# Written-out sequence loops, statistics further ahead in the first and last stage, and a re-placed bias scaling and normalisation in the second attention

## The chip, the cores and the metric

One core of a Trainium2 chip runs the whole program. TensorE (PE) multiplies and transposes, VectorE (DVE), ScalarE (ACT) and GpSimd (POOL) do elementwise work and reductions, SyncE (SP) issues most of the DMAs. Each engine runs its own instruction stream in order; semaphores join them. The metric is the time of one execution on the device in microseconds, the median of several.

## The reference

Sixteen sequences of 256 tokens with 256 features go through six residual steps of a decoder:

```python
x = x + _L0_attn_ref(_layernorm(x), ...)      # decaying linear attention
x = x + _L0_xattn_ref(_layernorm(x), ctx, ...)  # causal attention, 16 heads
x = x + _L0_ffn_ref(_layernorm(x), ...)       # 8 experts, 2 per token
x = x + _L1_attn_ref(_layernorm(x), ...)      # time mix and channel mix
x = x + _L1_xattn_ref(_layernorm(x), ctx, ctx, fside, ...)
x = x + _L1_ffn_ref(_layernorm(x), weight, bias)
```

The second attention adds a bias to its scores, and the last step multiplies in 8-bit precision:

```python
scores = jnp.einsum('bhqd,bhkd->bhqk', Q, K) * SCALE
scores = scores + lambda_bias * bias_struct[:, None, :, :]
attn = jax.nn.softmax(scores, axis=-1)
...
x_mat = quantize_e4m3(x2d, SCALE).astype(jnp.float16)
w_mat = quantize_e4m3(weight, SCALE).astype(jnp.float16)
out2d = (x_mat @ w_mat.T).astype(jnp.float32) * (SCALE * SCALE) + bias
```

`_layernorm` subtracts the mean and divides by the root of variance + 1e-5; the first step also divides its output by the root of its mean square.

## The kernel before

X, all 16 sequences, stays on the chip from the first stage to the last: 128 partitions by 32 tiles of 256 features, two tiles per sequence. Each of six functions is one stage (`decay_attention`, names `dec_`; `causal_attention`, `xa_`; `experts_ffn`, `moe_`; `time_channel_mix`, `mix_`; `biased_attention`, `xb_`; `float8_ffn`, `ffn_`), begun by a barrier of all engines. There is no planner: the order on each engine is the order in which the code stands, and every wait is written out as a semaphore and a count. b is the sequence, s = b % 2 its buffer.

**Loops.** The generator `turns` (L123) gives the sequences to each engine: sequence 0 is written out, then a device loop `Fori` runs over pairs, and the last ones are written out again (three, for the stages below). `long_turns` (L449) does the same for the two attentions: 0 and 1 and the last two are written out, six passes of the loop take 2 to 13. Inside a device loop, counts and addresses come from registers.

**First stage.** VectorE's turn b: `norm(b + 2)` (L112), `scan(b + 1)` (L406), the copy of the sums of squares of b (L425), `measure(b + 3)` (statistics L95, aggregation L98), then, when GpSimd's root `rms` is there, the addition into X (L430). GpSimd computes the roots in two steps (`inverse_root`, L104 an addition, L106 a power): first that of `rms`, then that of the statistics, `rstd`. Statistics and roots have one buffer, so `norm(b + 3)` of the next turn needs the root of what was measured in this one. TensorE turns the input (L321), sums squares (L332) and projects (L336).

**Second attention.** A turn has four steps g of four units (a unit is two heads of a block of 128 queries). TensorE: `scores` of step g (L1271), one or two jobs for the next sequence on the shared bank `p_a` (turn context, turn x, project keys, queries, values), `turn_unit` of the four units of the step before (L1283), `sum_units` (L1301). VectorE: per unit `shift_unit` (L1510: subtracts the scaled bias `neg` and finds the extreme, two operations each with its read of the result), `copy_unit` (L1519), and the closings: `normalise` (L1527, L1531: gives `xb_o` and frees `p_a`, for which TensorE waits at step 3 before `project_values`, L1237), `measure` and `norm` of the sequence after next at step 2, `finish_keys`, `finish_values` (L1496). ScalarE: exponentials (L1436) and copies. `prepare` on GpSimd (L1186) makes `neg` from the loaded bias, one sequence ahead; `add` (L1191) puts the result into X.

**Last stage.** VectorE first quantises the weight in twelve steps (L2765 to L2776); TensorE turns it, ScalarE copies it. Then VectorE's turn b: `norm(b + 2)` (L2786, waits for the root), `quantise(b + 2)` (two casts, L2790 and L2793), `measure(b + 3)`, and the bias addition for b (L2810). GpSimd's turn: the root of b + 3, then the addition of b into X (L2691). TensorE turns the quantised input (L2707) and multiplies (L2716); ScalarE reads both (L2738, L2745). Four DMAs write X out as sequences 4, 9, 13 and 15 are added.

## Time and profile before

| | us |
|---|---|
| median of 3 runs (2154.88 to 2162.77) | 2159.51 |
| the profiled execution | 2163.67 |
| its span | 2161.6 |
| `dec`, 0 to 109.2 | 109.2 |
| `xa`, to 450.0 | 340.8 |
| `moe`, to 1085.0 | 635.0 |
| `mix`, to 1581.5 | 496.5 |
| `xb`, to 2061.9 | 480.4 |
| `ffn`, to the end | 99.7 |

Busy times over the span: PE 1737.4 us (80%), DVE 1265.4 (59%), ACT 1116.1 (52%), POOL 591.5 (27%). In `xb` PE is busy for 427.8 of 480.4 us; in `ffn` for 26.5 of 99.7, at a granted clock of 0.50, with DVE busy for 67.3 and POOL for 38.4. A busy share of the whole span says little here, since each stage has its own limit; stage by stage one reads the timeline of an engine, where the number in brackets is the time that the engine was idle before the row and what ended that.

### The profile page before, as it was taken

The numbers are of one execution on the slowest core, as the hardware profiler recorded it, in microseconds if no ns is written. First come the engines' busy times: TensorE is split into PE (matmuls) and PEld (weight loads), VectorE is DVE, ScalarE is ACT, GpSimd is POOL, SyncE is SP. The second block draws the span as 40 slices with busy tenths as digits, with TensorE's granted clock in tenths as the row PEclk, the third lists the DMA queues.
The fourth block names the chain that finished last, engine by engine and source line by source line (L and its number), as shares of the span: only waits on it lengthen the run. The fifth ranks groups of instructions, "written<-read, shape, count | busy, mean of one in ns | idle before, by whom it ended". The sixth has DMA issues, their size and how long they took to land. (4 is left out here: it accounts for less than half of the span.)

```text
span 2161.6 us, 44295 instructions
## 1 busy us (share of the span) xinstructions
PE 1737.4 (80%) x13555; PEld 1431.1 (66%) x13555; DVE 1265.4 (59%) x4307; ACT 1116.1 (52%) x2535; POOL 591.5 (27%) x752
## 2 busy tenths in 40 slices
PE   4747777755599999999926999999958999999822
PEld 3625555545488888889915777777737777777711
DVE  4759998846410110101118999999618777778656
ACT  1259999931122222223325666666518888888712
POOL 2333233221211111101024666666410111111024
PEclk9879999965699999999967999999969999999955
...
DMA packets 112598, 153.61 MB, mean 71 GB/s; under 512 B 11449, under 2 KB 96769, under 8 KB 112353
## 3 DMA queue, kind: packets, MB, share of 16 engines
...
## 5 line engine op out<-in xcount | busy, mean ns | idle before, releaser
L1895 ACT ACTIVATE moe_hT<-moe_p_h,moe_b 128x256 f32<-128x256 f32 (+1 forms) x344 | 131.8, 434 | 370.8 <-PE moe_p_h L1845 370.6
L1845 PE MATMUL moe_p_h<-moe_gT,moe_w 128*128 128x256 f32 (+1 forms) x1376 | 256.9, 345 | 0.8 <-issue 0.8
L1855 PE MATMUL moe_p_y<-moe_w,moe_hT 128*128 128x256 f32 x1136 | 252.3, 379 | 0.0
L1845 PEld LDWEIGHTS moe_p_h<-moe_gT,moe_w 128*128 128x128 f32 x1376 | 228.2, 192 | 25.9 <-issue 1.2
L1436 ACT ACTIVATE xb_pr<-xb_sc,xb_nmax 128x256 f32<-128x256 f32 x512 | 225.5, 502 | 25.3 <-DVE xb_nmax L1510 23.2
L1855 PEld LDWEIGHTS moe_p_y<-moe_w,moe_hT 128*128 128x128 f32 x1136 | 212.5, 190 | 27.1
L1510 DVE CUSTOM_DVE_ANT_0 xb_sc<-xb_p_s,xb_neg 128x256 f32<-128x256 f32 x512 | 186.4, 420 | 69.6 <-PE xb_p_s L1271 56.8
L893 ACT ACTIVATE xa_pr<-xa_sc,xa_nmax 128x256 f32<-128x256 f32 (+1 forms) x512 | 204.5, 456 | 2.9 <-DVE xa_nmax L975 2.3
...
L2025 DVE COPY moe_gT<-moe_p_t 128x512 f32<-128x512 f32 (+1 forms) x43 | 25.7, 599 | 235.9 <-PE moe_p_t L1832 235.9
L2036 DVE TENSOR_TENSOR moe_gy<-moe_p_y,moe_b 128x256 f32<-128x256 f32 x71 | 27.5, 421 | 229.0 <-PE moe_p_y L1855 229.0
L975 DVE CUSTOM_DVE_ANT_0 xa_sc<-xa_p_s,xa_neg 128x256 f32<-128x256 f32 (+1 forms) x512 | 151.7, 352 | 15.8 <-PE xa_p_s L712 14.2
L1283 PE MATMUL xb_p_p<-xb_ident,xb_pr 128*128 128x128 f32 x1024 | 133.7, 274 | 6.6 <-DVE xb_prT L1519 6.5
L724 PE MATMUL xa_p_p<-xa_ident,xa_pr 128*128 128x128 f32 x768 | 120.4, 281 | 13.5 <-DVE xa_prT L984 6.0
L1283 PEld LDWEIGHTS xb_p_p<-xb_ident,xb_pr 128*128 128x128 f32 x1024 | 117.4, 141 | 16.3 <-ACT xb_pr L1436 8.1
L2300 PE MATMUL mix_p_kv<-mix_fv,mix_hid_sq 128*128 128x256 f32 x512 | 115.7, 379 | 1.7 <-ACT mix_hid_sq L2464 1.7
L2347 PE MATMUL mix_p_h<-mix_mixed,mix_fk 128*128 128x256 f32 x512 | 113.9, 381 | 0.0
L724 PEld LDWEIGHTS xa_p_p<-xa_ident,xa_pr 128*128 128x128 f32 x768 | 84.4, 143 | 34.7 <-ACT xa_pr L893 17.6
L2347 PEld LDWEIGHTS mix_p_h<-mix_mixed,mix_fk 128*128 128x128 f32 x512 | 98.0, 191 | 13.5
L2300 PEld LDWEIGHTS mix_p_kv<-mix_fv,mix_hid_sq 128*128 128x128 f32 x512 | 96.0, 190 | 14.5 <-ACT mix_hid_sq L2464 2.1
L1519 DVE COPY xb_prT<-xb_p_p 128x512 f32<-128x512 f32 x128 | 87.6, 684 | 1.7 <-PE xb_p_p L1283 1.7
L1415 ACT ACTIVATE xb_prT<-xb_p_p 128x512 f32<-128x512 f32 x128 | 75.3, 589 | 14.6 <-PE xb_p_p L1283 13.5
...
## 6 DMA issues: line engine op xcount, KB each, us to landing
...
```

The costliest lines, as they stand in the source:

```text
L724: last = pe.transpose(p_p[m % 2][:, (e * TB + kt) * P:(e * TB + kt + 1) * P], pr[:, m % RB, e, kt * P:(kt + 1) * P], ident[:, :])
L893: last = act.activation(pr[:, n % RB, e, 0:width], sc[:, n % RB, e, 0:width], ACT.Exp, bias=nmax[:, n % RB, e:e + 1], scale=-1.0)
L975: last = dve.tensor_tensor_reduce(out=sc[:, n % RB, e, 0:keys(t)], in0=scored_in(n, e), in1=neg[:, s, t, 0:keys(t)], scale=1.0, scalar=3e3 ...
L1283: last = pe.transpose(p_p[m % 2][:, (e * TB + kt) * P:(e * TB + kt + 1) * P], pr[:, m % RB, e, kt * P:(kt + 1) * P], ident[:, :])
L1436: last = act.activation(pr[:, n % RB, e, :], sc[:, n % RB, e, :], ACT.Exp, bias=nmax[:, n % RB, e:e + 1], scale=-1.0)
L1510: last = dve.tensor_tensor_reduce(out=sc[:, n % RB, e, :], in0=scored_in(n, e), in1=neg[:, s, t, :], scale=1.0, scalar=3e38, op0=ALU.add, ...
L1519: dve.tensor_copy(*turned_unit(m)).then_inc(s_["p_copied_v"], 1)
L1845: last = pe.matmul(p_h[n % 3][:, k * width:(k + 1) * width], w1[:, r, ic, (2 * n + k) * P:(2 * n + k + 1) * P], gT[:, r % 2, ic, 0:width], ...
L1855: last = pe.matmul(p_y[:, t * D:(t + 1) * D], hT[:, hc, t * P:(t + 1) * P], w2[:, r, hc, :], start=(hc == 0), stop=(hc == HC - 1))
L1895: last = act.activation(hT[:, 2 * n + k, 0:width], p_h[n % 3][:, k * width:(k + 1) * width], ACT.Gelu, bias=b1[:, bass.ds(e * HC + 2 * n + ...
L2300: last = pe.matmul(p_kv[:, t * D:(t + 1) * D], hid_sq[:, hc, t * P:(t + 1) * P], fv[:, hc, :], start=(hc == 0), stop=(hc == HC - 1))
L2347: last = pe.matmul(p_h[m % 2][:, k * S:(k + 1) * S], fk[:, ic, (2 * m + k) * P:(2 * m + k + 1) * P], mixed2[:, 0, ic, :], start=(ic == 0), ...
```

## The change

1. `turns` and `long_turns` no longer use a device loop: every sequence is written out on every engine, in all stages. A new generator `far_turns` does the same for the first and last stage.
2. First stage: statistics, roots and sums have two buffers, `measure` and its root are four sequences ahead instead of three, and the addition of b - 1 stands at the head of turn b.
3. Second attention: `prepare` moves from GpSimd to VectorE, to step 2; `normalise` of the first half stands after one unit of step 3 instead of two; `norm` moves from the end of step 2 to step 3, ahead of `finish_values`.
4. Last stage: `norm` moves from VectorE to ScalarE (one activation per tile with scale and shift); VectorE's `measure` also adds epsilon and negates the mean (two small operations), GpSimd takes the power and multiplies (no addition of epsilon), four sequences ahead, after its addition into X instead of before it. The weight is quantised after the first four measurements and two quantisations; its transposes go to the bank `p_y0`.

```diff
 def turns(eng, drain=False, ahead=1):
 
-
-
-    after = 1 if ahead == 1 else 3
-    yield 0, 0, 0
-    with eng.Fori(0, (B - 1 - after) // 2) as i:
-        yield 2 * i + 1, i, 1
-        yield 2 * i + 2, i + 1, 0
-    for b in range(B - after, B + drain):
+    for b in range(B + drain):
         yield b, b // 2, b % 2
 
 
...
@@ -202,6 +188,12 @@
 def columns(vec):
 
     return vec.rearrange("(c p) -> p c", p=P)
+
+
+def far_turns(eng, drain=0):
+
+    for b in range(B + drain):
+        yield b, b // 2, b % 2
...
+                norm_root(n, n % 2)
+            for b, h, s in far_turns(pool):
                 wait_alone(pool, stood_p, (sum_sq_ready, b + 1))
-                inverse_root(pool, rms[:, :], sum_sq[:, :], 1.0 / D, 1e-6, minus_half[:, :], mean_eps, rms_ready, b, stood_p)
-                if has_next(b, 3):
-                    norm_root(b + 3)
+                inverse_root(pool, rms[:, s, :], sum_sq[:, s, :], 1.0 / D, 1e-6, minus_half[:, :], mean_eps, rms_ready, b, stood_p)
+                if has_next(b, 4):
+                    norm_root(b + 4, s)
 
         @block.tensor
...
-            for q in range(4):
+            def add(n, s):
+                dve.wait_ge(rms_ready, n + 1 + HEAD)
+                for t in range(TB):
+                    last = dve.scalar_tensor_tensor(tile_of(X, n, t), p_y[s][:, t * D:(t + 1) * D], rms[:, s, t:t + 1],
+                                                    tile_of(X, n, t), ALU.mult, ALU.add)
+                last.then_inc(added, 1)
...
-            measure(0)
-            norm(0, 0)
-            measure(1)
-            norm(1, 1)
-            measure(2)
-            scan(0, 0)
             chain.close()
-            for b, h, s in turns(dve, ahead=3):
+            for b, h, s in far_turns(dve, drain=1):
+                if not first(b):
+                    add(b - 1, 1 - s)
                 if has_next(b, 2):
                     norm(b + 2, s)
                 if has_next(b):
                     scan(b + 1, 1 - s)
-                dve.wait_ge(y_ready, b + 1 + HEAD)
-                dve.tensor_copy(sum_sq[:, :], p_m[s][:, 0:TB]).then_inc(sum_sq_ready, 1)
-                if has_next(b, 3):
-                    measure(b + 3)
-                dve.wait_ge(rms_ready, b + 1 + HEAD)
-                for t in range(TB):
-                    last = dve.scalar_tensor_tensor(tile_of(X, b, t), p_y[s][:, t * D:(t + 1) * D], rms[:, t:t + 1],
-                                                    tile_of(X, b, t), ALU.mult, ALU.add)
-                last.then_inc(added, 1)
+                if not (isinstance(b, int) and b == B):
+                    dve.wait_ge(y_ready, b + 1 + HEAD)
+                    dve.tensor_copy(sum_sq[:, s, :], p_m[s][:, 0:TB]).then_inc(sum_sq_ready, 1)
+                if has_next(b, 4):
+                    measure(b + 4, s)
                 chain.close()
             dve.wait_ge(added, B + HEAD)
 
@@ -446,14 +443,9 @@
 STEPS = UNITS // STEP
 
 
-def long_turns(eng, drain):
-
-    yield 0, 0, 0
-    yield 1, 0, 1
-    with eng.Fori(0, (B - 4) // 2) as i:
-        yield 2 * i + 2, i + 1, 0
-        yield 2 * i + 3, i + 1, 1
-    for b in range(B - 2, B + drain):
+def long_turns(eng, drain=0):
+
+    for b in range(B + drain):
         yield b, b // 2, b % 2
 
 
...
 
-            def prepare(b, h, s):
-
-                pool.wait_ge(raw_in[s], 16 * h + 16)
-                if since(b, 2):
-                    pool.wait_ge(s_["shifted"], UNITS * (b - 1) + HEAD)
-                pool.sem_inc(s_["stood_p"], 1)
-                pool.tensor_scalar(neg[:, s, :, :], raw[:, s, :, :], lam_b[:, 0:1], None, ALU.mult).then_inc(s_["neg_ready"], 1)
...
@@ -1497,6 +1478,11 @@
                                              rows[:, 0, :].rearrange("p (h r) -> p h r", r=DH), ALU.add)
                 last.then_inc(s_["v_ready"], 1)
 
+            def prepare(n, h, s):
+
+                dve.wait_ge(raw_in[s], 16 * h + 16)
+                dve.tensor_scalar(neg[:, s, :, :], raw[:, s, :, :], lam_b[:, 0:1], None, ALU.mult).then_inc(s_["neg_ready"], 1)
+
             def shift_unit(b, s, n):
                 t = n // PAIRS
                 if n == 0:
@@ -1550,6 +1536,7 @@
             chain.done(dve.tensor_scalar(lam_b[:, :], lam_b[:, :], -1.0, None, ALU.mult))
             chain.wait()
             dve.sem_inc(s_["consts"], 1)
+            prepare(0, 0, 0)
             measure(0)
             norm(0)
             finish_keys(0, 0)
@@ -1564,9 +1551,10 @@
                         normalise(b - 1, 0)
                     if runs(b):
                         shift_unit(b, s, STEP * g)
-                        shift_unit(b, s, STEP * g + 1)
                     if g == 3 and since(b, 1):
                         normalise(b - 1, 1)
+                    if runs(b):
+                        shift_unit(b, s, STEP * g + 1)
                     if m is not None:
                         copy_unit(b, m)
                     if runs(b):
@@ -1578,12 +1566,14 @@
                         finish_keys(b + 1, 1 - s)
                     if g == 2 and has_next(b, 2):
                         measure(b + 2)
+                    if g == 2 and has_next(b):
+                        prepare(b + 1, h + s, 1 - s)
+                    if g == 3 and has_next(b, 2):
+                        norm(b + 2)
                     if g == 3 and has_next(b):
                         finish_values(b + 1, 1 - s)
                     if m is not None:
                         copy_unit(b, m + 2)
-                    if g == 2 and has_next(b, 2):
-                        norm(b + 2)
                 chain.close()
             dve.wait_ge(s_["added"], B + HEAD)
...
-            def norm_root(n):
+            def norm_root(n, s):
                 wait_alone(pool, s_["stood_p"], (s_["measured"], n + 1))
-                inverse_root(pool, rstd[:, :], aggr[:, :, 1], 1.0, LN_EPS, minus_half[:, :], s_["var_eps"], s_["rstd_ready"], n, s_["stood_p"])
...
-            for b, h, s in turns(pool, ahead=3):
-                if has_next(b, 3):
-                    norm_root(b + 3)
+                pool.tensor_tensor(scale[:, s, :], scale[:, s, :], minus_half[:, :], ALU.pow).then_inc(s_["rooted"], 1)
+                wait_alone(pool, s_["stood_p"], (s_["rooted"], n + 1))
+                pool.tensor_tensor(shift[:, s, :], scale[:, s, :], mean[:, s, :], ALU.mult).then_inc(s_["scaled"], 1)
+
+            for n in range(4):
+                norm_root(n, n % 2)
+            for b, h, s in far_turns(pool):
                 pool.wait_ge(s_["biased"], b + 1 + HEAD)
                 pool.tensor_tensor(X[:, bass.ds(TB * b, TB), :], y[:, s, :, :], X[:, bass.ds(TB * b, TB), :], ALU.add).then_inc(s_["added"], 1)
+                if has_next(b, 4):
+                    norm_root(b + 4, s)
...
+            def norm(n, s):
+                act.wait_ge(s_["scaled"], n + 1 + HEAD)
+                if not isinstance(n, int) or n >= 2:
+                    act.wait_ge(s_["quantised"], n - 1 + HEAD)
+                for t in range(TB):
+                    last = act.activation(xn[:, s, t, :], tile_of(X, n, t), ACT.Identity, scale=scale[:, s, t:t + 1], bias=shift[:, s, t:t + 1])
+                last.then_inc(s_["normed"], 1)
...
+            norm(0, 0)
+            norm(1, 1)
             read_input(0, 0)
             read_input(1, 1)
+            norm(2, 0)
+            act.wait_ge(s_["w_turned"], 1 + HEAD)
+            act.activation(flat(wt[:, :, :]), p_w, ACT.Copy).then_inc(s_["wt_ready"], 1)
             read_product(0, 0)
-            for b, h, s in turns(act, ahead=3):
+            for b, h, s in far_turns(act):
+                if has_next(b, 3):
+                    norm(b + 3, 1 - s)
                 if has_next(b):
                     read_product(b + 1, 1 - s)
...
+            def measure(n, s):
+                for t in range(TB):
+                    chain.done(dve.bn_stats(stats[:, s, t, :], tile_of(X, n, t)))
+                chain.wait()
+                for t in range(TB):
+                    chain.done(dve.bn_aggr(aggr[:, t, :], stats[:, s, t, :]))
+                chain.wait()
+                if not isinstance(n, int) or n >= 2:
+                    dve.wait_ge(s_["normed"], n - 1 + HEAD)
+                    dve.sem_inc(s_["stood_v"], 1)
+                chain.done(dve.tensor_scalar(scale[:, s, :], aggr[:, :, 1], LN_EPS, None, ALU.add))
+                dve.tensor_scalar(mean[:, s, :], aggr[:, :, 0], -1.0, None, ALU.mult).then_inc(s_["measured"], 1)
+
+            def quantise(n, s):
+                wait_alone(dve, s_["stood_v"], (s_["normed"], n + 1))
+                step(dve.tensor_copy(x8[:, s, :, :], xn[:, s, :, :], saturate=False))
+                if not first(n):
+                    wait_alone(dve, s_["stood_v"], (s_["turned_x"], n - 1))
+                dve.tensor_copy(xq[:, s, :, :], x8[:, s, :, :]).then_inc(s_["quantised"], 1)
+
+            measure(0, 0)
+            measure(1, 1)
+            quantise(0, 0)
+            quantise(1, 1)
+            measure(2, 0)
+            measure(3, 1)
+            quantise_weight()
             chain.close()
...
-            for b, h, s in turns(dve, ahead=3):
+            for b, h, s in far_turns(dve):
                 if has_next(b, 2):
-                    norm(b + 2)
                     quantise(b + 2, s)
-                if has_next(b, 3):
-                    measure(b + 3)
                 dve.wait_ge(s_["y_read"], b + 1 + HEAD)
                 if not first(b):
                     dve.wait_ge(s_["added"], b - 1 + HEAD)
                 last = dve.tensor_tensor(y[:, s, :, :], y16[:, s, :, :], bias[:, :].unsqueeze(1).broadcast_to([P, TB, D]), ALU.add)
                 last.then_inc(s_["biased"], 1)
+                if has_next(b, 4):
+                    measure(b + 4, s)
                 chain.close()
             dve.wait_ge(s_["added"], B + HEAD)
```

The instruction streams at three places. VectorE in the last stage, turn of sequence 0, before:

```order
L2786 TENSOR_SCALAR ffn_xn<-X,ffn_aggr,ffn_rstd 128x256 x2
L2790 CAST ffn_x<-ffn_xn 128x512
L2793 CAST ffn_xq<-ffn_x 128x512
L95 BN_STATS ffn_stats<-X 128x6 x2
L98 BN_AGGR ffn_aggr<-ffn_stats 128x2 x2
L2810 TENSOR_TENSOR ffn_y<-ffn_y,ffn_bias 128x512
L52 ISA
```

and after (line numbers of the changed kernel):

```order
L2800 CAST ffn_x<-ffn_xn 128x512
L2803 CAST ffn_xq<-ffn_x 128x512
L2819 TENSOR_TENSOR ffn_y<-ffn_y,ffn_bias 128x512
L2787 BN_STATS ffn_stats<-X 128x6 x2
L2790 BN_AGGR ffn_aggr<-ffn_stats 128x2 x2
L2795 TENSOR_SCALAR ffn_scale<-ffn_aggr 128x2
L2796 TENSOR_SCALAR ffn_mean<-ffn_aggr 128x2
L52 ISA
```

The normalisation is gone, two small operations are new, and the statistics moved behind the bias addition.

VectorE in the second attention, from the end of step 2 into step 3 of a turn (the four `p_s` are the score banks of one pair of units, `p_p` a bank of turned probabilities), before:

```order
L95 BN_STATS xb_stats<-X 128x6 x2
L98 BN_AGGR xb_aggr<-xb_stats 128x2 x2
L1519 COPY xb_prT<-xb_p_p0 128x512
L112 TENSOR_SCALAR xb_xn<-X,xb_aggr,xb_rstd 128x256 x2
L1510 ISA xb_sc,xb_nmax<-xb_p_s0,xb_neg 128x256
...
L1510 ISA xb_sc,xb_nmax<-xb_p_s3,xb_neg 128x256
L1510 ISA xb_nmax 128x1
L1527 RECIPROCAL xb_inv<-xb_p_a 128x16
L1531 TENSOR_TENSOR xb_o<-xb_p_a,xb_inv 128x2x4x16 x2
```

and after:

```order
L95 BN_STATS xb_stats<-X 128x6 x2
L98 BN_AGGR xb_aggr<-xb_stats 128x2 x2
L1484 TENSOR_SCALAR xb_neg<-xb_raw,xb_lam_b 128x512
L1505 COPY xb_prT<-xb_p_p0 128x512
L1496 ISA xb_sc,xb_nmax<-xb_p_s0,xb_neg 128x256
...
L1496 ISA xb_sc,xb_nmax<-xb_p_s1,xb_neg 128x256
L1496 ISA xb_nmax 128x1
L1513 RECIPROCAL xb_inv<-xb_p_a 128x16
L1517 TENSOR_TENSOR xb_o<-xb_p_a,xb_inv 128x2x4x16 x2
```

`xb_o` now comes after two score operations instead of four, `neg` is made here, and the normalisation into `xb_xn` stands ten rows further down, ahead of `xb_v`.

GpSimd in the last stage, a turn of the loop, before:

```order
L104 TENSOR_SCALAR ffn_rstd<-ffn_aggr 128x2
L106 TENSOR_TENSOR ffn_rstd<-ffn_rstd,ffn_minus_half 128x2
L2690 REGISTER_ALU
L2691 ISA
L2691 TENSOR_TENSOR X<-ffn_y,X 128x512
```

and after:

```order
L2682 TENSOR_TENSOR X<-ffn_y,X 128x512
L2674 TENSOR_TENSOR ffn_scale<-ffn_scale,ffn_minus_half 128x2
L2676 TENSOR_TENSOR ffn_shift<-ffn_scale,ffn_mean 128x2
```

The addition now stands ahead of the root, the register instructions of the loop are gone. Counted in this listing (a matmul and its weight load as one), TensorE's program grows from 3866 to 8179 instructions and VectorE's from 2116 to 4521.

## Rows read from the trace of the kernel before

**Rows 1.** Timeline, last stage, VectorE: start us, us, engine line op out<-in [idle before]

```profile
2144.88 1.67 DVE L2786 TENSOR_SCALAR ffn_xn<-X,ffn_aggr,ffn_rstd 128x256 f32 x2 [0.97 <-POOL ffn_rstd L106]
2146.58 0.43 DVE L2790 CAST ffn_x<-ffn_xn 128x512 fp8e4<-128x512 f32 x1
...
2147.38 0.75 DVE L95 BATCH_NORM_STATS2 ffn_stats<-X 128x6 f32 x2
...
2148.33 0.66 DVE L2810 TENSOR_TENSOR ffn_y<-ffn_y,ffn_bias 128x512 f32<-128x512 f16 x1
2149.96 1.67 DVE L2786 TENSOR_SCALAR ffn_xn<-X,ffn_aggr,ffn_rstd 128x256 f32<-128x256 f32 x2 [0.97 <-POOL ffn_rstd L106]
```

**Rows 2.** Timeline, the same turn, GpSimd

```profile
2144.14 0.70 POOL L106 TENSOR_TENSOR ffn_rstd<-ffn_rstd,ffn_minus_half 128x2 f32<-128x2 f32 x1 [0.18 <-POOL ffn_rstd L104]
2144.82 1.26 POOL L2691 TENSOR_TENSOR X<-ffn_y,X 128x512 f32 x1
```

**Rows 3.** Timeline, VectorE, a small operation of the time mix

```profile
1125.71 0.17 DVE L2506 TENSOR_SCALAR mix_scale_x<-mix_aggr 128x2 f32<-128x2 f32 x1
```

**Rows 4.** Timeline, ScalarE, two activations of 128x256 in the first stage

```profile
37.21 0.84 ACT L365 ACTIVATE dec_v<-dec_p_t,dec_coef 128x256 f32<-128x256 f32 x2 [4.06 <-PE dec_p_t L321]
```

**Rows 5.** Timelines, start of the last stage, GpSimd and VectorE

```profile
2064.30 0.20 POOL L66 MEMSET ffn_ident<- 128x128 f32 x1 [2.42 <-POOLq L193]
...
2067.80 0.43 DVE L2765 TENSOR_SCALAR ffn_w_nat<-ffn_w_nat 128x512 f32<-128x512 f32 x1 [7.37 <-DMA ffn_bias<-in_L_ffn_bias_dram]
...
2074.62 0.75 DVE L95 BATCH_NORM_STATS2 ffn_stats<-X 128x6 f32<-128x256 f32 x2 [0.25 <-DVE ffn_w_q L2776]
...
2087.30 0.66 DVE L2810 TENSOR_TENSOR ffn_y<-ffn_y,ffn_bias 128x512 f32<-128x512 f16 x1
```

**Rows 6.** Waits of 1640 to 2062 (total us, times, longest), then TensorE's timeline

```profile
PE xb_p_a L1237 <- DVE xb_o L1531: 16.2, 14, 1.2
...
2016.45 1.99 PE L1237 MATMUL xb_p_a<-xb_w,xb_cT 128*128 128x256 f32 x8 [1.03 <-DVE xb_o L1531]
```

**Rows 7.** Timeline, second attention, VectorE, step 3 of sequence 14

```profile
2014.23 0.42 DVE L1510 CUSTOM_DVE_ANT_0 xb_sc<-xb_p_s,xb_neg 128x256 f32<-128x256 f32 x1 [2.07 <-PE xb_p_s L1271]
...
2015.61 0.25 DVE L1527 RECIPROCAL xb_inv<-xb_p_a 128x16 f32<-128x16 f32 x1
```

**Rows 8.** Timeline, ScalarE, one row per turn of the second attention

```profile
1941.12 0.60 ACT L1399 ACTIVATE xb_oT<-xb_p_a 128x512 f32<-128x512 f32 x1 [0.80 <-PE xb_p_a L1222]
...
1968.45 0.60 ACT L1399 ACTIVATE xb_oT<-xb_p_a 128x512 f32<-128x512 f32 x1 [0.80 <-PE xb_p_a L1222]
...
1995.31 0.60 ACT L1399 ACTIVATE xb_oT<-xb_p_a 128x512 f32<-128x512 f32 x1 [0.80 <-PE xb_p_a L1222]
...
2022.02 0.60 ACT L1399 ACTIVATE xb_oT<-xb_p_a 128x512 f32<-128x512 f32 x1 [0.80 <-PE xb_p_a L1222]
```

**Rows 9.** Timeline, VectorE, first operation behind a back edge of the loop

```profile
1941.73 0.42 DVE L1510 CUSTOM_DVE_ANT_0 xb_sc<-xb_p_s,xb_neg 128x256 f32<-128x256 f32 x1 [2.80 <-issue]
```

**Rows 10.** Timelines, first stage, VectorE (four rows) and TensorE

```profile
73.13 0.88 DVE L430 SCALAR_TENSOR_TENSOR X<-dec_p_y,dec_rms,X 128x256 f32 x2 [0.43 <-POOL dec_rms L106]
74.15 0.74 DVE L112 TENSOR_SCALAR dec_xn<-X,dec_aggr,dec_rstd 128x256 f32 x2
...
101.03 0.88 DVE L430 SCALAR_TENSOR_TENSOR X<-dec_p_y,dec_rms,X 128x256 f32<-128x256 f32 x2 [1.31 <-POOL dec_rms L106]
101.82 1.26 DVE L406 TENSOR_TENSOR_SCAN dec_o<-dec_lam,dec_v 128x256 f32<-128x256 f32 x2
...
77.87 3.43 PE L336 MATMUL dec_p_y<-dec_wt,dec_o 128*128 128x256 f32 x8
```

**Rows 11.** Timeline, ScalarE, one row per turn of the experts' gate

```profile
477.85 0.60 ACT L1870 ACTIVATE moe_xT<-moe_p_t 128x512 f32<-128x512 f32 x1 [2.86 <-PE moe_p_t L1786]
480.86 0.60 ACT L1870 ACTIVATE moe_xT<-moe_p_t 128x512 f32<-128x512 f32 x1 [2.42 <-PE moe_p_t L1786]
484.23 0.60 ACT L1870 ACTIVATE moe_xT<-moe_p_t 128x512 f32<-128x512 f32 x1 [2.77 <-PE moe_p_t L1786]
```

126 lines of the change are left out of this document (53 added, 73 removed).

## The prediction

> **What bounds the kernel now.** I read first the timelines of the last stage (`float8_ffn`, from 2061.9 us to the end), since the diff rewrites it most; then the waits of TensorE in the second attention and the timelines around its longest one; then the distance between turns in all stages that loop; last the first stage. No engine bounds the whole span. Each stage has its own chain, so I price each stage by itself.
>
> In the last stage a turn takes 5.08 us, from one normalisation on VectorE to the next (2144.88 to 2149.96) [rows 1]. VectorE is the engine that closes the cycle, though it works for little over half of a clean turn: it waits 0.97 us for GpSimd's root, and then its two normalisations take 1.67 us instead of the 0.74 that two such take in the first stage [rows 10], because GpSimd's addition into X (1.26 us from 2144.82) runs beside them [rows 2]. So the cycle is statistics, power on GpSimd, addition on GpSimd, normalisation, casts.
>
> In the second attention TensorE is the busiest. Its one regular wait for VectorE is that of the value projection for `xb_o`: 14 times, 16.2 us in all, so 1.16 us each, and 1.03 us in the turn of sequence 14, where VectorE has no normalisation to do [rows 6]. VectorE did four score operations (2014.23 to 2015.61, so 1.38 us) before it began `normalise` [rows 7].
>
> Loops cost at their back edge: VectorE's first score operation after the branch starts 2.80 us late, put down to issue [rows 9]; the turn over that edge takes 27.33 us against 26.86 for the other (1941.12, 1968.45, 1995.31) [rows 8].
>
> **Last stage: the steady turn.** The normalisation leaves VectorE for ScalarE. VectorE keeps per turn: two casts, 0.80 us (2146.58 to 2147.38); statistics and aggregation, 0.95 (2147.38 to 2148.33); the bias addition, 0.66 [rows 1]; and it gains two operations on two columns, 0.17 each [rows 3]. That is 2.75 us. For the extra wait on the aggregation, the wait before the casts and the closing of the chain I add 0.25 (estimate). GpSimd's addition now starts right after the bias addition; it takes 1.26, the statistics beside it 0.95, so the small operations can be held 0.3 us more. I take the middle, 3.2 us.
>
> Who waits for whom then: GpSimd does the 1.26 addition, the power (0.70) [rows 2] and a small product, some 2.7 us at most if the product takes as long as the power: below 3.2. ScalarE gets two activations of 128x256, 0.84 for two [rows 4], beside two reads of 128x512, 0.60 each as in [rows 8]: 2.0 us. The statistics are four sequences ahead, so root and normalisation (about 1.3 + 0.9) have a whole VectorE turn before the casts ask for them. In ScalarE's queue the normalisation of b+3 stands ahead of the product of b+1; if the root is late both wait, but the bias addition of b+1 comes a turn later. So VectorE sets the pace by its own work. Twelve turns at 5.08 - 3.2 = 1.9 us give **22.6 us**. Bounds: 2.75 a turn (28.0), and 4.4 a turn if the casts too wait out a whole addition of 1.26 (8.2).
>
> Here a rule speaks against the sum. The trace shows the exclusion: 1.67 us for 0.74 of work beside the addition. The Trainium skill (page "SBUF — State Buffer", section "SBUF: two separate sides") says that the port pair shared by VectorE and GpSimd is "an **exclusive lock**, not a bandwidth split", taken by VectorE in its two-port modes or with two SBUF inputs. By it the casts, the small operations and the bias addition can all be held, and GpSimd by them; where they meet each other in each turn the pace is the rival's 4.4, not 3.2.
>
> **Last stage: start and end.** Now VectorE first waits for the weight (2067.80), quantises it, then prepares sequences 0 to 2; the first bias addition is at 2087.30 [rows 5]. After the change it starts with statistics when the stage begins (GpSimd's first operation: 2064.30 [rows 5]): two statistics with their small operations, 2.7 us; root and ScalarE until about 2067.9; both quantisations to 2070; two more statistics to 2072.8; the weight, the same 6.8 us (2067.80 to the first statistics at 2074.62) [rows 5], to 2079.6; then transposes, ScalarE's copy, the product and its read, some 3 us (estimate). First bias addition: 2082.6, so **4.7 us** earlier. The last three turns, which measure nothing, and what follows them stay. Last stage: 27.3, bounds 12 and 33.
>
> **Second attention.** (a) `normalise` stands one unit earlier, so 1.38/2 = 0.69 us earlier for 14 waits: 9.7 us. (b) The normalisation of x leaves the end of step 2, so the score operations of step 3 start when the scores are there, in all turns as in that of sequence 14: 1.16 - 1.03 = 0.13, 13 times: 1.7 us. (c) The bias scaling comes to VectorE: 0.43 us for 128x512 (the clamp of the weight, same form [rows 5]), 15 times, at the end of step 2. There VectorE waited for scores anyway (2.07 us idle at 2014.23 [rows 7]) and the wait for the root that it replaces is gone: nothing. Without that cover it would be 6.5 us. (d) What is late next: the normalisation of x (0.65) now stands ahead of the value read and a copy in step 3, and these end about 0.5 us later while TensorE comes 0.8 earlier. Counted from VectorE's first score operation of step 3: units, `normalise`, two copies, normalisation and value read end at 6.1 us (0.34 for each of eight score operations [rows 7], the rest an estimate of 3.3), and TensorE, 0.7 earlier, asks for the copy at about 6.9 (estimate: 1.99 for the projection [rows 6], the transposes, sums and scores behind it 3.4). It just holds. (e) Back edges: six passes, five jumps, 0.47 each [rows 8]: 2.3 us. Sum **13.7 us**; bounds 6 (half of a and b lost to d, one e) and 15.
>
> **First stage.** The order on VectorE within a turn stays; only the statistics used by the normalisation are one turn older. Two additions are followed by the next operation after 1.02 us when that is a normalisation (73.13, 74.15), and after 0.79 when it is a scan (101.03, 101.82) [rows 10]: the wait for the root is 0.23 us a turn. In every second turn it is hidden, because TensorE's projection ran at half clock (3.43 us for eight matmuls of 256 columns at 77.87 [rows 10], 0.43 each). Six turns at 0.23 are 1.4; the head gets some 0.6; the jumps some 1. I take **3 us**; bounds 1 and 8 (the latter if the denser turns keep 2.4 GHz and all 13 turns go at VectorE's pace).
>
> **Loops elsewhere.** `turns` is shared, so all stages are written out, not the two named. In the gate stage the turn over the edge takes 3.37 against 3.01 (480.86, 484.23; 477.85) [rows 11]: 0.36 for six, **2.2 us**. For the first attention and the time mix I take 0.5 together (0 to 2.5, five edges of 0.47).
>
> The Trainium skill (page "Runtime: NRT & Kernel Launch", section "Instruction fetch mechanics") says "Branching breaks sequential prefetch": a jump out of the window fetches its page first. The late start of 2.80 us at the edge agrees with it [rows 9].
>
> **Sum.** 27.3 + 13.7 + 3 + 2.2 + 0.5 = 46.7 us. The profiled execution took 2163.67 us (span 2161.6 and 2.1 around it): 2117. It is 4.2 us above the median of the three runs, 2159.51, and that is what I predict against: **2113 us**.
>
> **Rivals.**
> 1. *The lock.* In the last stage VectorE and GpSimd hold each other every turn; 4.4 us a turn. For it: the 1.67 us [rows 1]. Against: statistics, not casts, lie beside the addition in the new order. Gain 46.7 - 14.4 = 32.3: 2127 us.
> 2. *The attention's wait moves.* TensorE waits for the copy or the value read behind the normalisation of x instead of `xb_o`. For it: the margin of 0.8 us is the difference of two long sums. Half of 11.4 is lost: 2119 us.
> 3. *Slower: code fetch.* Written-out code is never run twice, so every block is fetched once; TensorE's program grows from 3866 to 8179 instructions, VectorE's from 2116 to 4521. If each of the 72 turns that were looped paid twice what the back edge costs once (0.94 us), that is 68 us: 2113 + 68 = 2181. It decides from 46.7/72 = 0.65 us a turn. Against: the turn of sequence 14 is written out already and takes 26.71 us (1995.31 to 2022.02), less than the looped 26.86 [rows 8].
> 4. *The clock in the first stage stays at 2.4 GHz*: 5 us more, 2108 us.
>
> **Chances.** Forecast 0.60 (2108 to 2118), rival 1 0.17, rival 2 0.12, rival 3 0.04, rival 4 0.07. The range 2103 to 2130 takes in 1, 2 and 4 and leaves out rival 3 and the far ends. A measurement of this kernel can tell about 0.3% (6.5 us) from no change. Only rival 3, or 1, 2 and several small losses at once, come near it: faster 0.94, same 0.03, slower 0.03.
>
> **What would show it.** Last stage: bias additions 3.2 us apart, no idle before the casts; wrong if they stand at 4 or more with casts of over 1 us. Second attention: turns of 25.9 to 26.0 us all alike, TensorE's wait for `xb_o` near 0.3 us; wrong if TensorE waits instead for a copy of the turned probabilities. Gate turns all at 3.0. First stage: no wait between addition and normalisation. The prediction fails if idle time put down to issue appears in stretches that had no jump.

## The result and the profile after

The changed kernel takes 2096.1 us (median; 2092.1 to 2105.1), the kernel before 2160.1 beside it: ratio 0.971, 95% interval 0.968 to 0.975. The gain is 64 us where 46.7 were forecast, and the time lies below the range (2103 to 2130). The profiled execution took 2094.1 us, 69.6 less than the profiled one of before (that one lay 3.6 us above its median, this one 2.0 below). First the page of the changed kernel, its busy times and the granted clock in 40 slices:

```profile
span 2092.3 us, 41326 instructions
PE 1713.1 (82%) x13555; PEld 1422.8 (68%) x13555; DVE 1247.0 (60%) x4323; ACT 1129.2 (54%) x2567; POOL 563.7 (27%) x736
PEclk9979999975699999999976999999998999999985
```

Where the 69.6 us lie, by stage, each from the start of its first operation to the start of its last in the two traces (us):

| stage | before | after | gain | forecast |
|---|---|---|---|---|
| first | 105.6 | 96.2 | 9.4 | 3 |
| first attention | 343.0 | 341.1 | 1.9 | 0.5 with the time mix |
| gate and experts | 621.0 | 617.0 | 4.0 | 2.2 |
| time mix | 486.4 | 481.5 | 4.9 | |
| second attention | 470.3 | 448.1 | 22.2 | 13.7 |
| last | 92.4 | 65.2 | 27.2 | 27.3 |

The gaps between the stages did not change. The last stage is the forecast almost to the tenth, in part by luck: the twelve turns gave 21.5 us for the 22.6 forecast, the start 4.6 for 4.7, and the end, which was to stay, gave 1.0. Its timeline, VectorE, GpSimd and ScalarE over one turn (start us, us, engine line operation out<-in, idle before), against [rows 1, 2]:

```profile
2063.15 0.43 DVE L2803 CAST ffn_xq<-ffn_x 128x512 bf16<-128x512 fp8e4 x1 [0.17 <-DVE ffn_x L2800]
2063.49 0.68 DVE L2819 TENSOR_TENSOR ffn_y<-ffn_y,ffn_bias 128x512 f32<-128x512 f16 x1
2064.09 0.74 DVE L2787 BATCH_NORM_STATS2 ffn_stats<-X 128x6 f32<-128x256 f32 x2
2064.87 0.25 DVE L2790 BATCH_NORM_AGGREGATE ffn_aggr<-ffn_stats 128x2 f32<-128x6 f32 x2
2065.30 0.25 DVE L2795 TENSOR_SCALAR ffn_scale<-ffn_aggr 128x2 f32<-128x2 f32 x1 [0.18 <-DVE ffn_aggr L2790]
2065.46 0.15 DVE L2796 TENSOR_SCALAR ffn_mean<-ffn_aggr 128x2 f32<-128x2 f32 x1
2065.79 0.43 DVE L2800 CAST ffn_x<-ffn_xn 128x512 fp8e4<-128x512 f32 x1 [0.18 <-DVE ffn_scale L2795]
...
2066.74 0.68 DVE L2819 TENSOR_TENSOR ffn_y<-ffn_y,ffn_bias 128x512 f32<-128x512 f16 x1
...
2064.25 1.27 POOL L2682 TENSOR_TENSOR X<-ffn_y,X 128x512 f32<-128x512 f32 x1
2065.80 1.06 POOL L2674 TENSOR_TENSOR ffn_scale<-ffn_scale,ffn_minus_half 128x2 f32<-128x2 f32 x1 [0.28 <-DVE ffn_mean L2796]
2067.03 0.44 POOL L2676 TENSOR_TENSOR ffn_shift<-ffn_scale,ffn_mean 128x2 f32<-128x2 f32 x1 [0.18 <-POOL ffn_scale L2674]
...
2067.51 1.09 ACT L2728 ACTIVATE ffn_xn<-X,ffn_shift,ffn_scale 128x256 f32<-128x256 f32 x2 [1.19 <-POOL ffn_shift L2676]
```

Bias additions stand 3.25 us apart in ten of the twelve turns (3.40 and 3.60 in the others; forecast 3.2). The casts run in 0.43 us. It is GpSimd that is held: its power (the root, 128x2) takes 1.06 us beside the casts, and took 0.70 before [rows 2]. The first bias addition comes 18.4 us after the stage's start instead of 23.0.

In the second attention, ScalarE's copy of the turned output (one per turn, against [rows 8]), then TensorE's value projection (against [rows 6]):

```profile
1929.94 0.60 ACT L1380 ACTIVATE xb_oT<-xb_p_a 128x512 f32<-128x512 f32 x1 [0.80 <-PE xb_p_a L1203]
1955.97 0.60 ACT L1380 ACTIVATE xb_oT<-xb_p_a 128x512 f32<-128x512 f32 x1 [0.80 <-PE xb_p_a L1203]
1982.01 0.60 ACT L1380 ACTIVATE xb_oT<-xb_p_a 128x512 f32<-128x512 f32 x1 [0.80 <-PE xb_p_a L1203]
...
1976.43 1.99 PE L1218 MATMUL xb_p_a<-xb_w,xb_cT 128*128 128x256 f32 x8 [0.34 <-DVE xb_o L1517]
```

The thirteen full turns take 26.02 or 26.03 us each (forecast 25.9 to 26.0), the wait for `xb_o` is 0.34 (forecast 0.3). These turns gave 12.7 of the 22.2 us. Another 7.6 came at the head of the stage, which here means the time up to ScalarE's first copy of the turned output (80.9 us, now 73.3); there the sum had nothing. And 1.8 came behind the last such copy (5.4 us, now 3.6).

### The profile page after: what moved, and what is told of

The parts are those of the page before. It is cut to its first block and busy times, and to the rows that moved or that the text cites. A ratio compares the mean times of both kernels' runs of the same rounds, so it can differ in the third digit from the quotient of the medians.

```text
span 2092.3 us, 41326 instructions
## 1 busy us (share of the span) xinstructions
PE 1713.1 (82%) x13555; PEld 1422.8 (68%) x13555; DVE 1247.0 (60%) x4323; ACT 1129.2 (54%) x2567; POOL 563.7 (27%) x736
## 3 DMA queue, kind: packets, MB, share of 16 engines
q8 instruction: 102, 1.67, 0.3%
```

## Experiments

Each kernel was profiled once, so the stage lengths and turns below are those of one execution. The time is the median of 2, 4 or 10 timed runs, the ratio is against runs of the kernel before beside them.

| kernel | first | first att. | gate, experts | time mix | second att. | last | time | ratio |
|---|---|---|---|---|---|---|---|---|
| before | 105.6 | 343.0 | 621.0 | 486.4 | 470.3 | 92.4 | 2160.1 | 1 |
| after | 96.2 | 341.1 | 617.0 | 481.5 | 448.1 | 65.2 | 2096.1 | 0.971 |
| loops_out | 108.5 | 341.5 | 617.2 | 481.0 | 462.8 | 92.3 | 2149.4 | 0.994 |
| loops_back | 96.2 | 343.0 | 620.4 | 484.9 | 453.3 | 64.8 | 2107.7 | 0.975 |
| only_first | 94.5 | 343.2 | 620.6 | 484.2 | 467.7 | 92.9 | 2147.5 | 0.994 |
| only_last | 109.1 | 343.1 | 620.2 | 486.5 | 471.6 | 64.9 | 2135.6 | 0.987 |
| before_busy | 100.8 | 343.0 | 620.2 | 485.0 | 462.9 | 92.4 | 2151.3 | 0.996 |
| measure_three | 105.6 | 342.2 | 617.2 | 480.6 | 452.7 | 65.2 | 2111.0 | 0.977 |
| normalise_back | 94.7 | 341.2 | 616.9 | 480.4 | 463.2 | 65.1 | 2105.9 | 0.974 |
| norm_back | 94.5 | 342.4 | 618.0 | 481.8 | 452.4 | 65.2 | 2101.5 | 0.972 |
| prepare_pool | 98.5 | 341.4 | 616.8 | 480.3 | 456.4 | 65.2 | 2101.4 | 0.972 |
| no_product | 95.9 | 341.4 | 617.0 | 480.3 | 453.8 | 64.5 | 2101.6 | 0.973 |
| fetch_first | 100.8 | 341.5 | 616.8 | 469.7 | 453.3 | 65.2 | 2089.2 | 0.966 |
| busy_fetch | 96.1 | 343.5 | 617.5 | 468.3 | 448.2 | 65.2 | 2086.8 | 0.966 |

**1. Loops written out, and nothing else.** `loops_out` is the kernel before with this edit:

```diff
-    after = 1 if ahead == 1 else 3
-    yield 0, 0, 0
-    with eng.Fori(0, (B - 1 - after) // 2) as i:
-        yield 2 * i + 1, i, 1
-        yield 2 * i + 2, i + 1, 0
-    for b in range(B - after, B + drain):
+    for b in range(B + drain):
         yield b, b // 2, b % 2
```

(and the same in `long_turns`); `loops_back` is the changed kernel with both loops back, which leaves its first and last stage written out. Expected:

> The kernel before, with its loops written out in all stages and nothing else changed. Theory A (the loops themselves cost what the changed kernel gained outside its edited lines): gate turns all 2.97 us and that stage 4 us shorter; time mix 5 us shorter, with some turns of 25.3 us among those of 26.5; first attention 2 us shorter; second attention 2.5 us shorter from its edges; last stage 2.5 us shorter; first stage 2 to 3 us shorter, turns still 4.6 to 5.4 us. Sum 18 us: 2142 us. Theory B (only back edges cost, the rest of the unforeseen gain comes with the edits or with the clock): mix turns stay at 26.5 us, sum 9 us: 2151 us. If the first stage already comes to 99 us here, its edit did nothing.

> The changed kernel with the device loops back in the four middle stages (both attentions, gate, time mix); first and last stage stay as changed. Theory A: 2 + 4 + 5 + 2.3 = 13 us slower than the changed kernel: 2109 us; mix turns all 26.5 us, second attention 26.0 us with 26.5 over each edge. Theory B: the middle stages lose only their edges, 2.3 + 2.2 + 0.5 = 5 us: 2101 us, and the mix keeps some turns of 25.3 us.

Measured: 12 us gained by the one (0.9944, interval 0.992 to 0.997), 11.7 lost by the other. Over the table, a stage that is written out is shorter in every kernel: time mix 480.3 to 481.8 against 484.2 to 486.5, first attention 341.1 to 342.4 against 343.0 to 343.2, gate and experts 616.8 to 618.0 against 620.2 to 621.0 (`fetch_first` and `busy_fetch` apart, whose edits touch two of these). Theory A holds there: some 4, 2 and 3.5 us where it expected 5, 2 and 4. It does not in the last stage (92.3 against 92.4): its turns are 5.08 us with the loop and without, so the waits of the turn hide it. The first stage (108.5) shows no gain either, but its granted clock stood at 1.2 GHz for 34.1 us here and for 20.5 in the trace of before, so the two cannot be compared. The theory's sum of 18 was too high.

In the second attention the edge did not cost 0.47 in every loop. VectorE's late start of 2.7 to 3.0 us behind the branch [rows 9] stands four times in the trace of before, five times in that of `only_last` and twice in that of `before_busy`. The longest turn over an edge takes 27.36, 27.51 and 27.19 us there. It stands in neither `only_first`, which has the same loop, nor `loops_back`, which loops over the new turn: turns of 26.93 and 26.86 us in the one, 26.11 and 26.03 in the other, so 0.08 for an edge. The three that show it have the first stage as it was before, ahead of this loop; the two that do not have it written out. Whether the place of the loop in the program decides was not tested. So (e) came true for this pair: the thirteen turns fell from 351.0 to 349.2 us in `loops_out`, 1.8 us, for 2.3 forecast. The Trainium skill (page "Runtime: NRT & Kernel Launch", section "Instruction fetch mechanics") has a taken branch break the prefetch when its target lies outside the window that is held; here such a late start stands behind the branch in three kernels and not in two, and none of them shows where the target lay.

**2. The first stage.** `only_first` is the kernel before with the new first stage. `before_busy` leaves all its order as it was and gives TensorE matmuls nobody reads:

```diff
                 if has_next(b, 2):
                     turn_input(b + 2, s)
+                for n_x in range(4):
+                    pe.transpose(p_x[:, n_x * P:(n_x + 1) * P], ident[:, :], ident[:, :])
...
             pe.wait_ge(s_["ident_ready"], 2 + HEAD)
+            for n_x in range(32):
+                pe.transpose(p_o[:, (n_x % 4) * P:(n_x % 4 + 1) * P], ident[:, :], ident[:, :])
             pe.wait_ge(s_["ones_set"], 1 + HEAD)
```

`measure_three` is the changed kernel with the statistics three ahead:

```diff
-                if has_next(b, 4):
-                    measure(b + 4, s)
+                if has_next(b, 3):
+                    measure(b + 3, 1 - s)
```

(the root on GpSimd likewise, and three measurements instead of four ahead of the turns). Expected:

> The kernel before with the new first stage alone (its edit and its written-out loop). Theory A (the root's wait gone and denser turns, so that TensorE keeps 2.4 GHz): the stage takes 97 to 99 us instead of 105.6, turns 4.05 us, granted clock 1.00 from 60 us on, and nothing else moves: 2151 us. Theory B (the gain of this stage was the clock's chance in one execution): turns of 4.6 to 5.4 us return in this execution and the stage takes 103 us: 2157 us.

> The kernel before with TensorE kept busy at two places by transposes of the identity into a bank nobody reads: four in each turn of the first stage (in the 1.2 us in which TensorE waits there), 32 at the head of the second attention (while it waits for its weights). No other edit. Theory C (what the changed kernel gained beyond the sum in the first stage and at the head of the second attention is the clock: 2.4 GHz kept instead of lost): the first stage shows no half-clock stretch after its head, its turns are 4.4 to 4.7 us, and it takes 98 to 101 us instead of 105.6 although it does more work; the second attention reaches its first output turn (ScalarE's copy of the transposed output) 74 us after its start instead of 80.9. Together 10 to 13 us less than before: 2149 us. Theory D (the edits' order and the loops do it, the clock follows): both stages as before or longer by the added transposes: 2163 us.

> The changed kernel with the statistics and their root of the first stage three sequences ahead again instead of four; the addition at the head of the turn and the two buffers stay. Forecast of the working: the root's wait of 0.23 us between addition and normalisation comes back, turns of 4.28 us instead of 4.05, stage about 98 us. Rival E: the ring that sets the turn is addition, normalisation, scan, copy, root; the place of the statistics costs more than the wait (turns of 4.4 us, as in the old stage at 2.4 GHz), and half-clock stretches return with the less dense turns, so that the stage takes 103 us or more.

The views by stretches from 60 us to the stage's end (the columns are stretch, us, busy time and instructions of PE, PEld, DVE, ACT and POOL, granted clock, DMA share, GB/s), of before, before_busy, after and measure_three in this order:

```profile
60.00:108.00 48.00, 38.97 (x200) 31.73 (x199) 34.56 (x98) 13.30 (x28) 16.66 (x38) 0.88 0.00 1
```

```profile
60.00:103.00 43.00, 36.64 (x232) 31.71 (x232) 32.39 (x93) 12.01 (x27) 15.97 (x37) 1.00 0.00 0
```

```profile
60.00:98.00 38.00, 30.41 (x182) 25.70 (x180) 29.97 (x87) 11.47 (x25) 14.64 (x32) 1.00 0.00 1
```

```profile
60.00:108.00 48.00, 41.27 (x189) 33.82 (x188) 33.16 (x95) 12.67 (x27) 16.41 (x37) 0.79 0.00 1
```

The same order with a busy TensorE keeps 2.4 GHz and is 4.8 us shorter (8.3 against `only_last`, which has the same old stage at 109.1), though it does more: turns of 4.34 and 4.64 us, from squares to squares on ScalarE, without the 5.2 to 5.7 of before. That is theory C. What the edit gives beyond it is the ring on VectorE, the closed chain of operations that sets the turn: `only_first` and `before_busy` both spend nothing of the stage at 1.2 GHz up to the last addition, and take 94.5 and 100.8 us, so the edit is worth 6.3. It does not secure the clock. Nine of these kernels have the new first stage, instruction for instruction, and their clock stood at 1.2 GHz in it for 0 us (three kernels, 94.5 to 94.7 us long), 6.8 (four, 95.9 to 96.2), 13.7 (`prepare_pool`, 98.5) and 20.5 (`fetch_first`, 100.8). The old order and `measure_three`, without added transposes, had 20.5 to 34.1 us.

Its timeline in `measure_three`, then in the changed kernel:

```profile
91.51 0.87 DVE L403 SCALAR_TENSOR_TENSOR X<-dec_p_y,dec_rms,X 128x256 f32<-128x256 f32 x2 [0.36 <-POOL dec_rms L106]
92.66 0.73 DVE L112 TENSOR_SCALAR dec_xn<-X,dec_aggr,dec_rstd 128x256 f32<-128x256 f32 x2 [0.28 <-POOL dec_rstd L106]
93.31 1.26 DVE L396 TENSOR_TENSOR_SCAN dec_o<-dec_lam,dec_v 128x256 f32<-128x256 f32 x2
94.50 0.13 DVE L426 COPY dec_sum_sq<-dec_p_m 128x2 f32<-128x2 f32 x1
```

```profile
83.55 0.88 DVE L403 SCALAR_TENSOR_TENSOR X<-dec_p_y,dec_rms,X 128x256 f32<-128x256 f32 x2 [0.35 <-POOL dec_rms L106]
84.34 0.73 DVE L112 TENSOR_SCALAR dec_xn<-X,dec_aggr,dec_rstd 128x256 f32<-128x256 f32 x2
84.99 1.26 DVE L396 TENSOR_TENSOR_SCAN dec_o<-dec_lam,dec_v 128x256 f32<-128x256 f32 x2
86.17 0.13 DVE L427 COPY dec_sum_sq<-dec_p_m 128x2 f32<-128x2 f32 x1
87.60 0.88 DVE L403 SCALAR_TENSOR_TENSOR X<-dec_p_y,dec_rms,X 128x256 f32<-128x256 f32 x2 [1.30 <-POOL dec_rms L106]
```

Addition, normalisation, scan, copy and the root on GpSimd follow each other in 4.05 us (83.55 to 87.60). The turn shown has no statistics any more, and the one before it, which has them, takes 4.05 us too, so these do not set the pace. With the statistics three ahead the normalisation starts 1.15 us after the addition instead of 0.79, a turn takes 4.42 at 2.4 GHz, the clock falls again (0.79), and the stage is back at 105.6 us. Rival E held, and the forecast of 4.28 did not. So the two buffers and the place of the addition give next to nothing without the fourth sequence: 4.42 us a turn against 4.49 on average in `before_busy`, both at 2.4 GHz.

**3. The last stage.** `only_last` is the kernel before with the new last stage. `no_product` leaves a part of the computation out (ScalarE then takes the negated mean as its bias, so the output is another):

```diff
-                pool.tensor_tensor(scale[:, s, :], scale[:, s, :], minus_half[:, :], ALU.pow).then_inc(s_["rooted"], 1)
-                wait_alone(pool, s_["stood_p"], (s_["rooted"], n + 1))
-                pool.tensor_tensor(shift[:, s, :], scale[:, s, :], mean[:, s, :], ALU.mult).then_inc(s_["scaled"], 1)
+                pool.tensor_tensor(scale[:, s, :], scale[:, s, :], minus_half[:, :], ALU.pow).then_inc(s_["scaled"], 1)
```

> The kernel before with the new last stage alone. Both theories: bias additions 3.25 us apart, the stage 70 us instead of 97, so 27 us less than before: 2132 us. If less than 24 us come, part of the changed kernel's 27 came from elsewhere.

> The changed kernel with GpSimd's small product left out in the last stage (the activation takes the negated mean as its bias, so this part of the computation is left out and the output changes). Forecast of the working (VectorE sets the pace by its own work and waits): bias additions stay 3.25 us apart, GpSimd idles 0.6 us more a turn. Rival: GpSimd's row of addition, power and product, 3.2 us with its waits, closes the turn together with VectorE; then the turn falls by 0.2 us or more.

The stage takes 64.9 us in `only_last`, and that kernel 26.5 less than the runs of before beside it (2162.1): all 27 us are the stage's own. Without the product the bias additions stay 3.25 us apart, and GpSimd's addition waits, where it had followed at once:

```profile
2065.20 1.27 POOL L2680 TENSOR_TENSOR X<-ffn_y,X 128x512 f32<-128x512 f32 x1 [0.64 <-DVE ffn_y L2817]
```

So VectorE sets the pace, by 2.7 us of work and three waits of 0.17 to 0.18 on its own results.

**4. The parts of the second attention.** From the changed kernel each edit is undone alone: `normalise_back` (the normalisation behind both units), `norm_back` (the normalisation of x at the end of step 2), `prepare_pool` (the bias scaling on GpSimd). The first:

```diff
                         shift_unit(b, s, STEP * g)
+                        shift_unit(b, s, STEP * g + 1)
                     if g == 3 and since(b, 1):
                         normalise(b - 1, 1)
-                    if runs(b):
-                        shift_unit(b, s, STEP * g + 1)
```

> The changed kernel with one edit of the second attention undone: the normalisation of the outputs' first half stands behind both units of step 3 again. Forecast of the working: TensorE asks for xb_o 0.69 us later at 14 places, turns of 26.72 us instead of 26.03, TensorE's wait for it 1.0 us instead of 0.34. Rival: the other two edits (scaling on VectorE, later normalisation of x) carry part of it and turns grow by less than 0.4 us.

> The changed kernel with the normalisation of x back at the end of step 2, behind the bias scaling that stays on VectorE. Forecast of the working: 0.13 us a turn (26.16 us). Rival: VectorE now has scaling (0.43) and normalisation (0.65) there, its score operations of step 3 start later, and turns grow by 0.5 us or more; then the place of the normalisation was priced too low and the cover for the scaling depends on it.

> The changed kernel with the bias scaling back on GpSimd. Forecast of the working: the move was worth nothing by itself, turns stay at 26.03 us. Rival: on GpSimd it delays the addition and the root behind it, or holds VectorE's operations beside it, and turns grow by 0.2 us or more; or VectorE is freed of 0.43 us on its path and turns fall by up to that.

Turns of 26.72, 26.17 and 26.03 us in this order, against 26.03: 0.69, 0.14 and nothing, as worked out. (`prepare_pool` is 8.3 us longer in this stage all the same, 6.8 of it at the head; of that below.) TensorE's wait for `xb_o` from 1640 us to the end of the stage (us in all, times, longest), in `normalise_back`, then `norm_back`:

```profile
PE xb_p_a L1218 <- DVE xb_o L1517: 14.4, 14, 1.0
```

```profile
PE xb_p_a L1218 <- DVE xb_o L1517: 6.8, 14, 0.6
```

The 7.6 us at the head follow the clock. The projection of the context, the first of the stage, in before, after and `before_busy`:

```profile
1604.31 3.50 PE L1229 MATMUL xb_p_a<-xb_cT,xb_w 128*128 128x256 f32 x8 [0.75 <-ACT xb_cT L1393]
```

```profile
1583.29 1.99 PE L1210 MATMUL xb_p_a<-xb_cT,xb_w 128*128 128x256 f32 x8 [0.75 <-ACT xb_cT L1374]
```

```profile
1594.24 1.99 PE L1232 MATMUL xb_p_a<-xb_cT,xb_w 128*128 128x256 f32 x8 [0.75 <-ACT xb_cT L1398]
```

The head in all kernels (us from the stage's start to the first output turn), and for how much of it the granted clock stood at 1.2 GHz:

| | after | busy_fetch | before_busy | norm_back | measure_three | loops_back | fetch_first | loops_out | no_product | normalise_back | prepare_pool | before | only_first | only_last |
|---|---|---|---|---|---|---|---|---|---|---|---|---|---|---|
| head | 73.3 | 73.5 | 73.8 | 74.1 | 76.4 | 76.6 | 77.0 | 77.2 | 77.3 | 78.1 | 80.1 | 80.9 | 81.9 | 82.4 |
| at 1.2 GHz | 13.8 | 10.5 | 11.3 | 14.4 | 21.8 | 21.9 | 25.4 | 21.5 | 25.2 | 25.1 | 35.4 | 30.9 | 36.3 | 36.9 |

The head follows the time at half clock, not the code: after, `measure_three`, `fetch_first` and `no_product` have the same instructions in this stage and heads of 73.3 to 77.3 us; `before_busy`, with the old order and its loops, has 73.8. At the start of the stage TensorE waits 18.5 us for its weights; with the transposes in that time, the clock is at 2.4 GHz when they are there (16 transposes of the weight in 1.94 us in `before_busy`, 3.34 after). Kernels with the old second attention and loops still stand at the long end (80.9 to 82.4), so whether the edits also shift the odds is open; of the 7.6 us, 4 lie within the spread of kernels with the same instructions. The changed kernel's profile has the shortest head of these four; against the other three the gain is 3.6 to 4.5 us.

The 1.8 us behind the last turn are such a spread too. The last product takes 3.78 us before and 1.99 after, but 3.66 in `measure_three` and 3.54 in `fetch_first`, with the same instructions as after. In the four timed runs of the changed kernel time and mean granted clock go together: 2092.1 us at 0.926, 2094.1 at 0.924, 2098.0 at 0.923, 2105.1 at 0.917.

**5. The time mix.** VectorE is busy for 89% of the turns (TensorE for 91%), and some of its operations last longer where GpSimd works beside them: a product of 128x256 that takes 0.47 us alone takes 1.49, and ends 0.3 us behind GpSimd's operation. I call it held. The turns of 26.5 us and those of 25.3, from ScalarE's `mix_xc` to the next, differ in which are held. VectorE of before, a turn of 26.54 us, and GpSimd's addition beside the last group:

```profile
1409.30 2.69 DVE L2479 SCALAR_TENSOR_TENSOR mix_mixed<-mix_dif,mix_vec,mix_xc 128x256 f32<-128x256 f32 x4 [0.26 <-DVE mix_dif L2608]
1412.51 0.68 DVE L2552 TENSOR_TENSOR mix_a<-mix_read,mix_den 128x512 f32<-128x512 f32 x1
1413.22 1.41 DVE L2554 TENSOR_TENSOR mix_a<-mix_a,mix_read 128x512 f32<-128x512 f32 x1
1418.05 3.47 DVE L2479 SCALAR_TENSOR_TENSOR mix_mixed<-mix_dif,mix_vec,mix_xa 128x256 f32<-128x256 f32 x6
...
1418.20 1.46 POOL L2206 TENSOR_TENSOR X<-X,mix_Y  x1
```

VectorE of the changed kernel, a turn of 25.32 us:

```profile
1337.81 1.67 DVE L2469 SCALAR_TENSOR_TENSOR mix_mixed<-mix_dif,mix_vec,mix_xc 128x256 f32<-128x256 f32 x4 [0.18 <-DVE mix_dif L2598]
1340.09 1.47 DVE L2542 TENSOR_TENSOR mix_a<-mix_read,mix_den 128x512 f32<-128x512 f32 x1
1341.60 0.69 DVE L2544 TENSOR_TENSOR mix_a<-mix_a,mix_read 128x512 f32<-128x512 f32 x1
1345.71 4.73 DVE L2469 SCALAR_TENSOR_TENSOR mix_mixed<-mix_dif,mix_vec,mix_xa 128x256 f32<-128x256 f32 x6
...
1357.24 2.69 DVE L2477 SCALAR_TENSOR_TENSOR X<-mix_got,wt,X 128x256 f32<-128x256 f32 x4 [0.89 <-DMA mix_got<-moe_rows_out,mix_which]
```

The group of four takes 2.69 or 1.67 us, the second product 1.41 or 0.69. Others go the other way (the first product 0.68 or 1.47, the group of six 3.47 or 4.73), and each of these two turns has four operations held. Over twelve turns (the second to the thirteenth) the sum counts, that is what VectorE's products and sums take beyond 0.48 us (128x256) or 0.69 (128x512), where it is more than 0.15:

| a turn, mean | before | loops_back | after | loops_out | measure_three | fetch_first |
|---|---|---|---|---|---|---|
| held, us | 3.70 | 3.59 | 3.45 | 3.33 | 3.22 | 2.26 |
| turn, us | 26.46 | 26.36 | 26.20 | 26.13 | 26.11 | 25.03 |

Looped kernels settle on 26.5 to 26.6 us in nearly every turn (10 or more of 13), written-out ones change between that, 25.3 and, less often, 27.3. Why the loop does it is not shown. The holding is the exclusion that the prediction feared in the last stage; the Trainium skill (page "SBUF — State Buffer", section "SBUF: two separate sides") has the lock taken by VectorE operations with two SBUF inputs against a GpSimd operation that reads SBUF, and these are such. To test it I moved GpSimd's addition away from the last group:

```diff
-                if not ended(b):
-                    add_y(b)
                 if has_next(b, 3):
                     fetch(b + 3, 1 - s)
+                if not ended(b):
+                    add_y(b)
```

(`fetch_first`), and in `busy_fetch` gave TensorE work at three heads too:

> The changed kernel with one new edit in the time mix: GpSimd fetches the rows of the next sequence before it adds the mixed values into X instead of after it. Lock theory (a turn of 26.5 us holds VectorE's products and sums to the end of a GpSimd operation beside them, 1.4 to 1.5 us instead of 0.47; which ones are held sets the turn, and looping kept the worse pattern): at least one 1.49 goes, turns fall to 25.3 us or less, the stage from 481.5 to about 470 us. Rival: other operations are held in its place, or another engine closes the turn, and turns stay between 25.3 and 26.5 us.

> The changed kernel with that edit and with TensorE kept busy at the heads of three stages by transposes of the identity nobody reads (40 in the first attention, 110 in the time mix, 32 in the second attention), while it waits for transfers. Clock theory: half-clock time at the heads falls, the second attention's first output turn comes 72 us after its start or earlier, the head of the time mix is 2 to 3 us shorter, the first attention's less than 1 us; 5 us less than the same kernel without the transposes. Rival: the heads wait for transfers, not for TensorE, and nothing is gained outside the second attention.

VectorE and GpSimd of `fetch_first`, a turn of 24.95 us:

```profile
1245.69 3.72 DVE L2469 SCALAR_TENSOR_TENSOR mix_mixed<-mix_dif,mix_vec,mix_xa 128x256 f32<-128x256 f32 x6
...
1256.16 1.79 DVE L2477 SCALAR_TENSOR_TENSOR X<-mix_got,wt,X 128x256 f32<-128x256 f32 x4
...
1254.09 1.28 POOL L2196 TENSOR_TENSOR X<-X,mix_Y 128x512 f32<-128x512 f32 x1
```

The group of six has 1 us less held than the 4.73, and the sum over `mix_got` nothing (2.69 after). Against the turn of 25.32 two operations fewer are held; for it VectorE waits 1.01 us for TensorE's `mix_p_k`. Turns of 24.95 to 25.2, the stage 469.7 us, 11.8 less, and 2089.2 us in all: faster than both kernels (0.966, interval 0.965 to 0.968). The lock theory holds: held time and turn fall by the same 1.2 us (the last column against after). The edit also brings the fetched rows sooner, and VectorE no longer waits for `mix_got` in this turn (0.89 in that of 25.32), but over the twelve turns its idle time is the same, 2.3 us a turn against 2.2, so that is not what shortened them. `busy_fetch` came to 2086.8, where 5 us less were expected; the 2.4 cannot be told from nothing. It is 3.5 us shorter at the head of the second attention, 1.9 at that of the time mix, and 2.0 longer at that of the first attention, where the transposes stand ahead of the work (that they delay it is argued, not tested).

## Why the prediction was wrong

*Right:* the last stage, turn (3.25 for 3.2) and start (4.6 for 4.7), with 1.1 us too much for its turns and 1.0 too little for its end; rivals 1 and 3 fell (casts of 0.43, no idle put down to issue on VectorE in the second attention). In the second attention (a), (b) and (c) each measured by itself: 0.69, 0.14, 0 a turn, (e) gave 1.8 us for 2.3, and in the full turns TensorE waits for no copy behind the normalisation (rival 2).

*Wrong, by terms:*

1. **First stage, 3 us taken; 9.4 here (the old form takes 105.6 to 109.1 us over the kernels, the new one 94.5 to 100.8).** The step that failed is "In every second turn it is hidden, because TensorE's projection ran at half clock": it took the clock of one trace as given, and with it let the order count for the root's wait alone, six times. With no time at 1.2 GHz in either, the new order is 6.3 us shorter (94.5 against 100.8): 4.05 a turn instead of 4.49, and some at the start. The other 3.1 of the 9.4 are clock: 6.8 us at 1.2 GHz in this trace of the new stage, 20.5 in that of the old. That part can come out otherwise; with 20.5 in both (`fetch_first`) the gain is 4.8. I had the other case as rival 4 with 0.07, and priced it at VectorE's old pace. The root's wait was undersized too: 0.23 from one row pair, 0.37 a turn by `measure_three`, and the 4.05 us of the ring are below all I allowed.
2. **Loops elsewhere, 2.7 taken; 10.8 here, 10.7 by `loops_out`, 8.7 by `loops_back`.** I priced only what a back edge shows in one turn, and gave the time mix and the first attention 0.5 together without a reason. In the time mix the turns of before, 26.5 to 26.6 us, are alike because VectorE is held in the same places each time. In the first attention all turns fall, from 19.87 and 19.79 to 19.70, not only those over an edge. In the gate they fall from 3.37 and 3.01 to 2.98. Conversely (e) in the second attention, 0.47 an edge, is 0.08 in `only_first` and `loops_back`.
3. **Head and end of the second attention, nothing taken; 7.6 and 1.8 here.** The sum compared turns and left out that TensorE starts the stage's work at 1.2 GHz, and that the time at that level in the head differs between kernels by up to 26 us (10.5 to 36.9), by 11.6 with the same instructions. No edit there can be credited with all of this gain: heads with the same instructions differ by 4 us, ends by 1.8.

Term 2 is shown by runs, though not why a loop lengthens turns that cross no edge. For 1 and 3 runs show the part of the clock and that transposes nobody reads restore it; how much of that part this comparison got is partly chance. The lower end of the range, 2103, left room for rival 4 (5 us) but not for the loops and the clock at the head beside it.
